# Front of a gated-loop layer: phase angles by Ln, Exp and a Newton step, integer phases, and another order of the stages ahead of the expert tiles

## The chip, the cores and the metric

The kernel runs on one core of one Trainium2 chip. The metric is the time of one execution on the device in microseconds (us), as the median of several runs. A core has five engines that work side by side, each with an instruction stream of its own: PE (matrix products into PSUM banks), DVE (vector work), ACT (activation functions, copies), POOL (vector work and, here, the issue of gathers and scatters) and SP (the issue of other DMAs). They wait for each other by semaphores. ACT keeps a table of functions; where the next function isn't in it, the program has an instruction ACT_TABLE_LOAD.

## The reference, cut to what matters

Two layers over 2048 tokens of 128 numbers. Each adds to its input an attention part and a feed-forward part, both of the normed input. The change touches the first layer alone.

```python
# first layer, attention: xn is the normed, scaled input of one sequence of 512 tokens
q = xn @ wq; k = xn @ wk; v = xn @ wv; a = xn @ wa; g = xn @ wg
a_r, a_i = jnp.split(a, 2, axis=-1)
a_c = lax.complex(a_r, a_i)
magnitude = jax.nn.sigmoid(jnp.abs(a_c))
phase = jnp.angle(a_c)
a_c = magnitude * jnp.exp(1j * phase)
# y[t] = a_c[t] * y[t-1] + k[t] * v[t], over the sequence
y = q * jnp.real(y)
y = y * jax.nn.silu(g)
return y @ wo
# first layer, feed-forward: two of eight experts for every token
h1 = x_rep @ w1[e].T
a, g = jnp.split(h1, 2, axis=-1)
he = jax.nn.silu(a) * g @ w2[e].T
out = out * scores.reshape(-1, 1)
combined = out.reshape(N, TOP_K, h).sum(axis=1)
# second layer: a state-space scan and 64 experts, eight for every token
```

## The kernel before, in words

The tokens lie in NB = 4 blocks of TB = 512, one sequence each; a tile of the attention is 128 features by 512 tokens. The kernel is written by engine: five functions (SP, POOL, ACT, DVE, PE) that each issue their instructions in the order of the text, with waits on counting semaphores. Tables of Python numbers say at which place a step stands: `PROJ` is the order of the 24 projections on PE with the PSUM bank of each, `FR_ACT` and `FR_DVE` count the steps of the front, `FR_BESIDE`, `BACK_AT` and `BACK_STEPS` say beside which tile of the loop a step of the attention is issued.

*The angle of a block.* PE makes the products ar and ai (L315 to L317, three matmuls each, since numbers are split in a high and a low part). ACT copies and squares both (L730 to L734), DVE adds the squares and bounds the sum (L1080, L1082), ACT takes the square root (L745), which is |a|, and Abs of ar (L742, L756). The angle is twice the arctangent of ai / (|a| + |ar|), turned by sign where ar is negative. DVE adds (L1091), takes the reciprocal in two halves (L1092, L1094) and multiplies (L1095). ACT then makes Sigmoid of |a| (L762) and Arctan (L763), `angle(b)`. DVE makes two numbers from the sign of ar (L1098, L1099) and from them and the arctangent the angle in turns, split in a part rounded to a fine grid and a rest (`turn`, L1102 to L1106). Both parts are summed along the sequence by scans in float (`whole` L1159, `rest` L1161); `wrap` (L1164 to L1166) takes whole turns off.

*The rest of the attention.* ACT makes sines of the phase in two steps (`sin` L770 to L772, `double` L774 and L776). DVE turns k * v back by the phase (`spin`), runs a real and an imaginary decay scan (`fall_i`, `fall_r`), turns the sum forward and multiplies it by q * silu(g) (`sum`); PE multiplies by wo; DVE adds (`add`). Block b begins these steps at tile `BACK_AT[b]` of the loop below.

*The experts.* From a routing table, 39 tiles of 128 token slots of one expert each are made. DVE writes one-hot tables, PE multiplies them: L1495 makes the table of tokens (32 products of 128x78), L1503, at step 5 of the second half of the projections, that of the weights (32 products of 128x117). DVE turns the first into row numbers (L1115 to L1120) and the second into `weight` (L1140 to L1142). Then the tile loop runs, n from -2. For each tile POOL gathers 128 rows by an indirect DMA (`fetch`, L563, ten tiles ahead), PE turns the rows (L1444), ACT copies the high part (L783), DVE takes the low part (L1190), PE makes the two halves of the hidden layer (L1455 to L1461), ACT takes Silu (`tile_silu`, L790), DVE multiplies (`gate`, L1198), PE turns the result (L1471), ACT copies it (L797), PE makes the output (L1482), ACT weighs it (`weigh_out`, L806) and POOL scatters it by an indirect DMA (`send`, L582). Four buffers t_out stand between ACT and POOL. From tile 27 on POOL prepares weights of the second layer in between (`prepare`). The second layer begins behind the last scatter.

*What the change touches around it.* In `angle`, blocks 0 and 1 come ahead of the first tile's Silu and blocks 2 and 3 at tile 14 (`ANGLES_AT`). POOL splits the projection weights first, then those of the experts, and spreads the lane numbers in two pieces between (`spread_lanes`, L548). It gathers five tiles, waits for the weights table, clears three pads and gathers five more.

## Time and profile before

| what | value |
|---|---|
| median of 3 runs | 439.59 us (439.34 to 443.05) |
| the profiled execution | 439.73 us |
| its span on the core | 437.98 us, shown as 438.0 |
| busy: PE, DVE, ACT, POOL | 331.7, 352.8, 263.1, 247.3 us |

The span is the time from the first instruction to the last on the core; 1.75 us of the execution lie outside it. Busy time is the sum over a whole span with stages of different kinds, so a share of it tells nothing of a stage. In a row of a timeline the first number is the start in us from the span's start, the second the duration; in brackets at the end stands how long the engine had been idle before, and what ended that wait.

### The profile page before, as it was taken

The numbers are of one execution on the slowest core, as the hardware profiler recorded it, in microseconds if no ns is written. First come the engines' busy times: TensorE is split into PE (matmuls) and PEld (weight loads), VectorE is DVE, ScalarE is ACT, GpSimd is POOL, SyncE is SP. The second block draws the span as 40 slices with busy tenths as digits, with TensorE's granted clock in tenths as the row PEclk, the third lists the DMA queues.
The fourth block names the chain that finished last, engine by engine and source line by source line (L and its number), as shares of the span: only waits on it lengthen the run. The fifth ranks groups of instructions, "written<-read, shape, count | busy, mean of one in ns | idle before, by whom it ended". The sixth has DMA issues, their size and how long they took to land. (4 is left out here: it accounts for less than half of the span.)

```text
span 438.0 us, 5588 instructions
## 1 busy us (share of the span) xinstructions
PE 331.7 (76%) x1491; PEld 233.4 (53%) x1491; DVE 352.8 (81%) x623; ACT 263.1 (60%) x443; POOL 247.3 (56%) x254
## 2 busy tenths in 40 slices
PE   0855698927798698989702986979798888988875
PEld 0535466717786596877601553535455554545453
DVE  5869999899799597959229677888999988988955
ACT  2477596072757657575512589768668578678320
POOL 5486602510587377778830000058988988889850
PEclk9996698675999799999955999899999999999999
DMA  6365300100111111311060002004778866755973
GB/s 174 91 186 139 82 0 8 36 18 0 38 44 49 31 43 49 91 46 36 25 204 6 1 1 48 0 7 91 138 149 159 159 130 136 150 109 103 180 151 96
DMA packets 36212, 35.09 MB, mean 80 GB/s; under 512 B 12165, under 2 KB 30838, under 8 KB 36182
## 3 DMA queue, kind: packets, MB, share of 16 engines
q0 software_dynamic: 7104, 21.90, 24.1%
q1 hardware_dynamic: 29078, 12.84, 10.9%
q8 instruction: 14, 0.23, 0.2%
q14 instruction: 16, 0.13, 0.1%
HBM read 13.29 MB, written 4.65 MB: 41 GB/s over the span
## 5 line engine op out<-in xcount | busy, mean ns | idle before, releaser
L1301 DVE TENSOR_TENSOR_SCAN state<-dec,win_t 128x1024 f32<-128x1024 f32 x32 | 83.7, 2637 | 2.4 <-ACT dec L862 1.4
L871 ACT ACTIVATE sil<-psum,vec_t 128x512 f32<-128x512 f32 x64 | 43.2, 687 | 44.3 <-PE psum L317 44.2
L635 POOL TENSOR_SCALAR state<-state,ssm_cb 128x1024 f32<-128x1024 f32 x32 | 63.2, 1975 | 2.5 <-POOL sel_now L612 2.5
L582 POOL DMA_INDIRECT parts<-t_out,part x39 | 41.0, 1052 | 40.0 <-ACT t_out L806 30.2
L563 POOL DMA_INDIRECT x_tile<-normed,token x39 | 41.3, 1059 | 32.5 <-DVEq L1120 20.3
L1630 PE MATMUL psum<-hid,g_w 128*128 128x512 f32 x128 | 59.5, 592 | 0.0
L1312 DVE TENSOR_TENSOR hid<-sil,psum 128x512 f32<-128x512 f32 x64 | 41.7, 677 | 14.5 <-ACT sil L871 8.2
L1622 PE MATMUL psum<-cw_hl,sel_now 128*128 128x512 f32 x64 | 36.6, 572 | 16.6 <-DVE hid L1312 13.9
L797 ACT ACTIVATE t_hid_t<-psum 128x384 f32<-128x384 f32 x39 | 19.2, 492 | 31.2 <-PE psum L1471 31.2
L622 POOL MEMSET dec<- 128x4 f32 x6 | 0.6, 104 | 64.2 <-DVEq L1269 50.4
L1198 DVE TENSOR_TENSOR t_hid<-t_sil,psum 128x352 f32<-128x352 f32 x39 | 20.3, 521 | 19.4 <-ACT t_sil L790 16.6
L1630 PEld LDWEIGHTS psum<-hid,g_w 128*128 128x128 f32 x128 | 24.2, 189 | 20.3 <-issue 18.0
L1482 PE MATMUL psum<-w_out,t_hid_t 128*128 x234 | 33.8, 282 | 1.1 <-ACT t_out L806 0.9
L642 POOL DMA_DIRECT2D xn_tok<-state x32 | 28.7, 898 | 10.2 <-POOL state L635 8.4
L862 ACT ACTIVATE dec<-dt_t,ssm_a 128x2044 f32<-128x2044 f32 x16 | 31.1, 1992 | 3.9 <-DVEq L1269 3.8
L1482 PEld LDWEIGHTS psum<-w_out,t_hid_t 128*128 128x128 f32 x234 | 30.2, 197 | 1.8 <-issue 1.7
L1444 PE MATMUL psum<-ident,x_tile 128*128 128x128 f32 x39 | 12.4, 317 | 23.2 <-DVE xt_lo L1190 21.1
L1622 PEld LDWEIGHTS psum<-cw_hl,sel_now 128*128 128x128 f32 x64 | 12.0, 188 | 31.9 <-DVE hid L1312 23.8
L315 PE MATMUL psum<-xn_hi,g_hi 128*128 128x512 f32 x64 | 25.8, 403 | 3.0 <-ACT sil L871 3.0
L316 PE MATMUL psum<-xn_hi,g_lo 128*128 128x512 f32 x64 | 25.3, 395 | 0.0
L317 PE MATMUL psum<-xn_lo,g_hi 128*128 128x512 f32 x64 | 25.2, 394 | 0.0
L1455 PE MATMUL psum<-w_hi,xt_hi 128*128 x78 | 25.0, 405 | 0.0
(316 smaller groups left out, 860.0 us busy)
## 6 DMA issues: line engine op xcount, KB each, us to landing
xn_tok<-state POOLq DMA_DIRECT2D x32, 512.0 KB, 4.7
e_raw<-in_L_ffn_w SPq DMA_DIRECT2D x16, 128.0 KB, 2.2
both<-parts SPq DMA_DIRECT2D x4, 512.0 KB, 5.1
e_raw<-in_L_ffn_w SPq DMA_DIRECT2D x8, 176.0 KB, 2.5
res<-in_L_attn_x SPq DMA_DIRECT2D x4, 256.0 KB, 3.5
normed<-rows SPq DMA_DIRECT2D x1, 1024.0 KB, 5.5
g_raw<-in_L_ffn_w SPq DMA_DIRECT2D x16, 64.0 KB, 2.2
g_w<-in_L_ffn_w SPq DMA_DIRECT2D x16, 64.0 KB, 2.4
```

What stands on the lines that cost most here:

```text
L315: pe.matmul(acc, w_hi, m_hi, start=True, stop=False)
L563: pool.indirect_dma_start(out=x_tile[n % XRING][:, :], out_offset=None, in_=normed, in_offset=bass.IndirectOffsetOnAxis(ap=token[:, n:n + ...
L582: pool.indirect_dma_start(out=parts, out_offset=bass.IndirectOffsetOnAxis(ap=part[:, n:n + 1], axis=0), in_=t_out[n % ORING][:, :], in_off ...
L635: own(pool.tensor_scalar(state[k % 4][:, :], state[k % 4][:, :], ssm_cb[:, k // 2:k // 2 + 1], 0.0, ALU.mult, ALU.add))
L642: pool.dma_start(y_t[:, (k % 2) * HALF:(k % 2 + 1) * HALF], state[k % 4][:, :], accum_op=ALU.add).then_inc(y_in[k % 4], 16)
L862: act.activation(dec[n % DECS][:, :].rearrange("p (b t) -> p b t", t=TB)[:, :, 1:TB], dt_t[:, :].rearrange("p (b t) -> p b t", t=TB)[:, :, ...
L871: act.activation(sil[c % SRING][:, :], ps[c % 2][:, :], ACT.Silu, bias=vec_t[:, V_B1 + c // NBLK:V_B1 + c // NBLK + 1]).then_inc(h_silu, 1)
L1301: dve.tensor_tensor_scan(state[k % 4][:, :], dec[(k // 2) % DECS][:, at_half], win_t[:, at_half], 0.0, ALU.mult, ALU.add).then_inc(scanned, 1)
L1312: dve.tensor_tensor(hid[c % HRING][:, :], sil[c % SRING][:, :], ps[2 + c % 2][:, :], ALU.mult).then_inc(hid_done, 1)
L1482: ins = pe.matmul(ps[O_BANK][:, 0:P], t_hid_t[n % 2][:, c * P:(c + 1) * P], w_out[:, e, c, :].rearrange("p a d -> p (a d)"), start=(c == 0 ...
L1622: pe.matmul(ps[2 + c % 2][:, :], sel_now[g % GRING][:, :], blk(cw_hl, tb), start=True, stop=True).then_inc(cwx_made, 1)
L1630: pe.matmul(ps[4 + tb][:, :], g_w2[g % GRING][:, :], hid[c % HRING][:, :], start=False, stop=g == NG - 1, skip_group_check=True).then_inc( ...
```

## The change

**Angles.** The reciprocal leaves DVE. DVE adds |ar| to |a| (`den`), ACT takes Ln and then Exp with a scale of -1 of the sum, block by block (`over`), and DVE makes one Newton step and the product (`tan`, three operations). All four Abs stand ahead of the square roots. The sign of ar is taken by ACT (Sign, with a tiny bias) instead of two DVE operations.

**Place of the angles.** All four blocks' Sigmoid and Arctan stand ahead of the first tile's Silu (n = -2 and -1); none is left at tile 14.

**Phases.** An angle is counted in 2^15 to a turn. The scan `whole` writes integers, `wrap` is a bitwise and and one more operation. The sine is taken as a shifted sine and its square in one ACT step of four operations; `spin`, `fall_i`, `fall_r`, `back` and `sum` on DVE have 8 operations for 9. The steps of a block's back part fall from 15 DVE operations to 12 and from 5 ACT operations to 4.

**Order and banks.** `PROJ` has another order: k and v of block 0 and k of block 1 come ahead of ar and ai of blocks 2 and 3, and q of block 3 goes to the bank that g of block 0 had. The weights table stands behind all projections. DVE makes the sums of squares and the token table ahead of the products of k and v, and the weights from the weights table (`leave_weights`) inside the tile loop at n = 0. ACT spreads the lane numbers in four pieces. POOL splits the projection weights behind expert 3 and gathers all ten tiles at once. Waits that stood ahead of the tile loop on PE stand inside it.

The diff, cut:

```diff
-                [("k", 2, 6), ("v", 2, 7), ("k", 3, 2), ("v", 3, 3), ("g", 1, 4), ("q", 1, 0), ("g", 2, 4), ("q", 2, 1),
-                 ("g", 3, 4), ("q", 3, 5)])
...
+                [("k", 2, 6), ("v", 2, 0), ("k", 3, 5), ("v", 3, 1), ("g", 1, 6), ("q", 1, 5), ("g", 2, 4), ("q", 2, 0),
+                 ("g", 3, 1), ("q", 3, 3)])
...
-        ANGLES_AT = 14
+        FR_ACT_AT = {-2: [("angle", 0), ("angle", 1)], -1: [("sign", 0), ("angle", 2), ("angle", 3)], 1: [("sign", 1)],
+                     2: [("sign", 2)], 4: [("sign", 3)]}
+        FR_BESIDE = {-2: [("tan", 2), ("q", 2)], -1: [("tan", 3), ("q", 3)], 0: [("turn", 0)], 3: [("turn", 1)],
+                     12: [("turn", 2)], 22: [("turn", 3)]}
...
-        BACK_OPS = {"whole": 1, "rest": 1, "wrap": 3, "spin": 2, "fall_i": 2, "fall_r": 2, "sum": 3, "add": 1}
+        BACK_OPS = {"whole": 1, "rest": 1, "wrap": 2, "spin": 2, "fall_i": 1, "fall_r": 1, "back": 2, "sum": 2, "add": 1}
...
-            pool.wait_ge(proj_in, 16 * 6)
-            split(proj_raw[:, :, :], proj_hi[:, :, :], proj_lo[:, :, :])
-            pool.nop().then_inc(weights_split, 1)
-            def spread_lanes(half):
...
-                if e in (LANES_AT, 3):
-                    pool.wait_ge(qkv_t_made, NBLK)
-                    spread_lanes(int(e == 3))
+                if e == 3:
+                    pool.wait_ge(proj_in, 16 * 6)
+                    split(proj_raw[:, :, :], proj_hi[:, :, :], proj_lo[:, :, :])
+                    pool.nop().then_inc(weights_split, 1)
...
-            for n in range(AHEAD // 2):
+            for n in range(AHEAD):
                 fetch(n)
...
+            def spread_lanes(n):
+
+                lo, hi = n * P // LANES, (n + 1) * P // LANES
+                own(act.activation(lane_p[:, lo:hi, :], lane[:, lo:hi, None].to_broadcast([P, P // LANES, NSEL]), ACT.Copy))
+                act.nop().then_inc(lanes_ready, 1)
...
-            step(act.activation(held["q"][0], held["ar"][0], ACT.Abs))
+            for b in BLOCKS:
+                step(act.activation(held["q"][b], held["ar"][b], ACT.Abs))
             for b in BLOCKS:
                 act.wait_ge(fr_dve, FR_DVE["m2", b])
                 step(act.activation(held["decay"][b], t1[b], ACT.Sqrt))
-            act.wait_ge(table_made, 1)
+            leave_key(2)
+            leave_key(3)
             for b in BLOCKS:
+                act.wait_ge(fr_dve, FR_DVE["den", b])
+                step(act.activation(held["q"][b], t1[b], ACT.Ln))
+                step(act.activation(held["q"][b], held["q"][b], ACT.Exp, scale=-1.0))
+            for b in BLOCKS:
+                act.wait_ge(fr_pe, FR_PE["g", b])
                 if b == 2:
-                    act.wait_ge(weights_made, 1)
-                act.wait_ge(fr_pe, FR_PE["g", b])
+                    act.wait_ge(weights_hot, 1)
                 step(act.activation(t2[b], ps[FR_BANK["g", b]][:, :], ACT.Silu))
...
+                    step(act.activation(t2[b], held["ar"][b], ACT.Sign, bias=least[:, 0:1]))
...
+                step(act.activation(turn_cos[:, :], th, ACT.Abs))
+                step(act.activation(turn_sin[:, :], th, ACT.Sin, scale=math.pi / TURN, bias=eighth[:, 0:1]))
+                step(act.activation(turn_sin[:, :], turn_sin[:, :], ACT.Square))
+                step(act.activation(k, turn_cos[:, :], ACT.Sin, scale=-2.0 * math.pi / TURN, bias=half_pi[:, 0:1]))
...
-                if n == ANGLES_AT:
-                    for b in (2, 3):
-                        angle(b)
+                for name, b in FR_ACT_AT.get(n, ()):
+                    angle(name, b)
...
+                    dve.wait_ge(fr_act, FR_ACT["over", b])
+                    step(dve.tensor_tensor(t1[b], t1[b], q, ALU.mult))
+                    step(dve.scalar_tensor_tensor(t1[b], t1[b], 2.0, q, ALU.subtract, ALU.mult))
+                    step(dve.tensor_tensor(t1[b], ai, t1[b], ALU.mult))
...
-                    step(dve.reciprocal(t1[b][:, half[0]], den[:, half[0]]))
...
-                    step(dve.tensor_tensor_scan(k, ones[:, :], ar, 0.0, ALU.mult, ALU.add))
+                    step(dve.tensor_tensor_scan(k.bitcast(mybir.dt.int32), ones[:, :], ar, 0.0, ALU.mult, ALU.add))
...
-                    step(dve.tensor_scalar(ar, k, ROUND_INT, ROUND_INT, ALU.add, ALU.subtract))
-                    step(dve.tensor_tensor(k, k, ar, ALU.subtract))
-                    step(dve.tensor_tensor(th, k, th, ALU.add))
+                    step(dve.tensor_scalar(whole, whole, int(TURN) - 1, None, ALU.bitwise_and))
+                    step(dve.scalar_tensor_tensor(th, whole, TURN / 2, th, ALU.subtract, ALU.subtract))
...
                 for name, b in FR_BESIDE.get(n, ()):
-                    turn_part(name, b)
+                    front(name, b)
+                if n == 0:
+                    leave_weights()
...
-            for at_step, (name, b, bank) in enumerate(PROJ[1]):
-                if at_step == WEIGHTS_AT:
-                    weights_table()
+            for name, b, bank in PROJ[1]:
                 project(name, b, bank)
+            pe.wait_ge(weights_hot, 1)
+            for c in range(NSEL):
+                ins = pe.matmul(ps[TABLE_BANK][:, 2 * NTILE:5 * NTILE], slot_hot[:, :, c], tile_hot[:, 0:3, :, c],
+                                start=c == 0, stop=c == NSEL - 1)
+            ins.then_inc(weights_made, 1)
```

What the diff doesn't show at once is where the table loads of ACT stand, which the compiled program decides. The instructions of ACT, before, from the square roots to the last Abs (`at_all` holds |a|, `for_front` and `front` the front's scratch, `kept` the attention's tiles, `xt_hi` a tile of rows):

```order
L745 ACT_TABLE_LOAD
L745 ACTIVATE at_all<-for_front 128x512 x4
L751 ACT_TABLE_LOAD
L751 ACTIVATE for_front<-psum 128x512
L738 ACTIVATE kept_51<-psum 128x512
L738 ACTIVATE kept_52<-psum 128x512
L751 ACTIVATE for_front<-psum 128x512
L751 ACTIVATE front_140<-psum 128x512 x2
L756 ACTIVATE front_140<-at_all 128x512 x3
L783 ACTIVATE xt_hi_66<-psum 128x128
```

The same place in the changed kernel, from the square roots on; the last row begins block 1, and blocks 1 to 3 have four rows like the four of block 0; behind them come a load and the four Silus:

```order
L751 ACT_TABLE_LOAD
L751 ACTIVATE at_all<-for_front 128x512 x4
L743 ACTIVATE kept_51<-psum 128x512
L743 ACTIVATE kept_52<-psum 128x512
L756 ACT_TABLE_LOAD
L756 ACTIVATE kept_93<-for_front 128x512
L757 ACT_TABLE_LOAD
L757 ACTIVATE kept_93<-kept_93 128x512
L756 ACT_TABLE_LOAD
```

Between the square roots and the Silus there was one load. Now eight more stand there, one ahead of each Ln (L756) and each Exp (L757), and all Silus are behind them.

PE, before, at the weights table (L1503) in the middle of the projections:

```order
L317 MATMUL psum<-xr_lo,proj_hi 128x512
L1503 MATMUL psum<-tile_hot,slot_hot 128x117 x32
L315 MATMUL psum<-xr_hi,proj_hi 128x512
L316 MATMUL psum<-xr_hi,proj_lo 128x512
L317 MATMUL psum<-xr_lo,proj_hi 128x512
```

PE, changed, the last projection, the weights table (L1512) and the first turn of a tile (L1448):

```order
L317 MATMUL psum<-xr_hi,proj_hi 128x512
L318 MATMUL psum<-xr_hi,proj_lo 128x512
L319 MATMUL psum<-xr_lo,proj_hi 128x512
L1512 MATMUL psum<-tile_hot,slot_hot 128x117 x32
L1439 TENSOR_LOAD tile_e
L1439 ISA x2
L1448 MATMUL psum<-ident,x_tile_54 128x128
```

The table stood between two projections with five more behind it; now it stands between the last projection and the first tile.

DVE, before, from the low part of tile 2 to the gating of tile 0 (L1198):

```order
L1190 TENSOR_TENSOR xt_lo_71<-psum,xt_hi_68 128x128
L1102 TENSOR_TENSOR for_front<-for_front,front_140 128x512
L1103 SCALAR_TENSOR_TENSOR for_front<-for_front 128x512
L1105 TENSOR_SCALAR at_all<-for_front 128x512
L1106 TENSOR_TENSOR at_all<-for_front,at_all 128x512
L1159 SCALAR_TENSOR_TENSOR turn_k_86<-ones,at_all 128x512
L1198 TENSOR_TENSOR t_hid_74<-t_sil_72,psum 128x352
```

DVE, changed, from the same low part to the same gating (now L1196):

```order
L1188 TENSOR_TENSOR xt_lo_71<-psum,xt_hi_68 128x128
L1098 SCALAR_TENSOR_TENSOR for_front<-front_140,for_front 128x512
L1100 TENSOR_SCALAR at_all<-for_front 128x512
L1101 SCALAR_TENSOR_TENSOR at_all<-at_all,for_front 128x512
L1102 SCALAR_TENSOR_TENSOR at_all<-front_140,at_all 128x512
L1142 SCALAR_TENSOR_TENSOR spare<-part_f,spare 128x39
L1143 SCALAR_TENSOR_TENSOR part<-part_f,spare 128x39
L1146 COPY weight<-psum 128x39
L1147 TENSOR_TENSOR weight<-weight,psum 128x39
L1148 TENSOR_TENSOR weight<-weight,psum 128x39
L1157 SCALAR_TENSOR_TENSOR turn_k_86<-ones,at_all 128x512
L1196 TENSOR_TENSOR t_hid_74<-t_sil_72,psum 128x352
```

The turn of block 1 gave way to that of block 0 (the turn of block 0 stood ahead of the low part before), and the five operations on the weights stand between it and the scan.

## Rows read from the trace of the kernel before

**Rows 1.** Windows: length, busy of PE, PEld, DVE, ACT, POOL; clock, DMA share, GB/s.

```profile
0.00:53.20 53.20, 26.82 (x143) 20.20 (x144) 40.95 (x139) 27.84 (x61) 34.39 (x46) 0.85 0.50 138
89.60:111.10 21.50, 12.94 (x52) 11.44 (x53) 19.80 (x31) 9.98 (x21) 0.48 (x1) 0.60 0.02 5
111.10:221.50 110.40, 91.76 (x607) 80.24 (x605) 82.61 (x142) 70.68 (x174) 82.04 (x76) 0.96 0.16 46
```

**Rows 2.** Groups of POOL from 111.1 to 221.5: scatters and gathers, idle time before.

```profile
L582 POOL DMA_INDIRECT parts<-t_out,part x39 | 41.0, 1052 | 40.0 <-ACT t_out L806 30.2 <-issue 8.2 <-POOL sw_lo L540 0.8
L563 POOL DMA_INDIRECT x_tile<-normed,token x29 | 31.4, 1083 | 9.0 <-issue 7.3 <-PE psum L1444 1.2 <-POOL ssm_cb L592 0.5
```

**Rows 3.** Waits of POOL: us in total, times, the longest.

```profile
POOL parts L582 <- ACT t_out L806: 30.2, 8, 21.1
```

**Rows 4.** Timeline of POOL: three of the 39 scatters.

```profile
111.16 1.00 POOL L582 DMA_INDIRECT parts<-t_out,part  x1 [21.07 <-ACT t_out L806]
...
148.68 1.19 POOL L582 DMA_INDIRECT parts<-t_out,part  x1 [4.00 <-ACT t_out L806]
...
220.51 0.97 POOL L582 DMA_INDIRECT parts<-t_out,part  x1 [0.31 <-issue]
```

**Rows 5.** Timeline of ACT at tile 14: both table loads.

```profile
141.91 1.28 ACT L762 ACT_TABLE_LOAD   x1
...
145.84 1.28 ACT L790 ACT_TABLE_LOAD   x1
```

**Rows 6.** Timeline of PE at the end of the front.

```profile
76.16 6.56 PE L1503 MATMUL psum<-tile_hot,slot_hot 128*128 128x117 bf16 x32 [1.11 <-DVEq L1129]
...
86.86 0.40 PE L315 MATMUL psum<-xr_hi,proj_hi 128*128 128x512 f32 x1
...
87.33 0.40 PE L317 MATMUL psum<-xr_lo,proj_hi 128*128 128x512 f32 x1
89.61 0.33 PE L1444 MATMUL psum<-ident,x_tile 128*128 128x128 f32 x1 [1.88 <-DVE front L1091]
```

**Rows 7.** Timeline of ACT in the front.

```profile
53.24 0.60 ACT L730 ACTIVATE at_all<-psum 128x512 f32<-128x512 f32 x1 [1.96 <-POOLq L554]
...
63.60 1.23 ACT L738 ACTIVATE kept<-psum 128x512 f32<-128x512 f32 x2
64.87 0.63 ACT L742 ACTIVATE kept<-at_all 128x512 f32<-128x512 f32 x1
67.91 1.28 ACT L745 ACT_TABLE_LOAD   x1 [2.41 <-DVE for_front L1082]
...
72.14 1.28 ACT L751 ACT_TABLE_LOAD   x1
73.43 0.60 ACT L751 ACTIVATE for_front<-psum 128x512 f32<-128x512 f32 x1
...
90.35 1.28 ACT L762 ACT_TABLE_LOAD   x1
...
98.39 0.46 ACT L790 ACTIVATE t_sil<-psum 128x352 f32<-128x352 f32 x1 [0.19 <-PE psum L1461]
```

**Rows 8.** Timeline of DVE: a reciprocal, a turn's operation, a scan, the first gating.

```profile
78.83 1.75 DVE L1092 RECIPROCAL for_front<-kept 128x256 f32<-128x256 f32 x1
...
96.57 0.69 DVE L1103 SCALAR_TENSOR_TENSOR for_front<-for_front 128x512 f32<-128x512 f32 x1
...
101.32 1.22 DVE L1159 TENSOR_TENSOR_SCAN turn_k<-ones,at_all 128x512 f32<-128x512 f32 x1
102.58 0.52 DVE L1198 TENSOR_TENSOR t_hid<-t_sil,psum 128x352 f32<-128x352 f32 x1
```

**Rows 9.** Timeline of ACT in the second layer: Exp, Square, a load ahead of Ln.

```profile
261.72 1.06 ACT L884 ACTIVATE pair<-pair 128x1024 f32<-128x1024 f32 x1
...
264.89 2.56 ACT L891 ACTIVATE at_all<-at_all,half_mid 128x512 f32<-128x512 f32 x4
267.46 1.28 ACT L894 ACT_TABLE_LOAD   x1
```

More of the change, by code:

```diff
@@ L15 @@
 TB = 512
-ROUND_TURN = 1.5 * 2.0 ** 10
+TURN = 2.0 ** 15
+QUARTER = TURN / 4
 ROUND_INT = 1.5 * 2.0 ** 23
@@ L364, in program @@
         BACK_AT = (0, 9, 19, 28)
[L365 to L367 removed]
+        BACK_STEPS = {"whole": 0, "rest": 1, "wrap": 2, "sin": 3, "spin": 4, "fall_i": 5, "fall_r": 6, "back": 7, "sum": 8,
+                      "wo": 9, "add": 10}
+        BACK_OPS = {"whole": 1, "rest": 1, "wrap": 2, "spin": 2, "fall_i": 1, "fall_r": 1, "back": 2, "sum": 2, "add": 1}
@@ new lines, in _ @@
+            for b in BLOCKS:
+                front("m2", b)
+            dve.wait_ge(table_made, 1)
+            of_lane, of_row = (ps[TABLE_BANK][:, n * NTILE:(n + 1) * NTILE] for n in range(2))
+            own(dve.tensor_copy(part_f[:, :], of_lane))
+            own(dve.scalar_tensor_tensor(part_f[:, :], of_row, float(P * TOPK), part_f[:, :], ALU.mult, ALU.add))
+            own(dve.tensor_scalar(token_f[:, :], part_f[:, :], -1.0, 0.5, ALU.min, ALU.mult))
+            own(dve.tensor_scalar(token_f[:, :], token_f[:, :], -0.25, ROUND_INT, ALU.add, ALU.add))
@@ L1063, in _ @@
+            own(dve.tensor_scalar(token[:, :], token_f[:, :], ROUND_INT - NTOK, None, ALU.subtract))
+            dve.nop().then_inc(token_ready, 1)
+            front("kv", 0)
+            front("kv", 1)
+            for b in BLOCKS:
+                front("den", b)
             own(dve.tensor_tensor_scan(counts[:, 0, :], ones[0:1, 0:NTILE], ones[0:1, 0:NTILE], 0.0, ALU.mult, ALU.add))
```

245 lines of the change are left out of this document (107 added, 138 removed).

## The prediction

> **What bounds the kernel now.** I read the stages first. The windows [rows 1] cut the span into a front to 53.2 us, a rest of the front, a first-tile stage from 89.6, the loop of 39 tiles from 111.1 to 221.5, and the second layer. In the loop POOL is busy for 82.04 of 110.4 us, in 76 instructions. PE is busier, so the next view is who waits for whom. POOL's groups [rows 2] show 39 scatters and 29 gathers, 1.05 and 1.08 us each, with a fixed gap of 0.30 us that the profile calls "issue" between nearly all of them. The waits [rows 3] show eight scatters that waited for ACT's t_out, 30.2 us in all, of which 21.1 is the first. The other seven took 9.1 us; 7 x 0.30 is the usual gap, so 7.0 us are true waiting. The timeline [rows 4] places 3.70 of it at 148.68 (4.00 less 0.30), behind the stall of ACT at 141.91: a table load, four angle instructions and a load back [rows 5]. So the loop is POOL's queue of issues: from the first scatter at 111.16 to the last at 220.51 are 109.35 us, of which 7.0 are waits for a late t_out and 102.35 are POOL's own.
>
> Ahead of it stands the front. PE's first turn of a tile begins at 89.61 [rows 6], ACT's first Silu of a tile at 98.39 [rows 7], the first gating multiply on DVE at 102.58 [rows 8], the first scatter at 111.16: 8.78, 4.19 and 8.58 us. In that stage the granted clock of PE averaged 0.60, so it ran mostly at its lower level of 1.2 GHz; in the loop it averaged 0.96, nearly all at 2.4 GHz [rows 1]. Whatever delays the first scatter delays the last, unless POOL's 7.0 us of waiting absorb it. The second layer follows the last scatter and isn't changed.
>
> **The change part by part, in the time of the trace.** *Start of the front.* POOL's two spreads go to ACT, in four Copies of 128x1024; the nearest row of that size takes 1.06 us [rows 9], so 4.2 us. ACT is busy for 27.84 of the first 53.2 us, and still waits 1.96 for POOL at 53.24 [rows 1, 7]. POOL's projection split moves behind expert 3, into time that the spreads free. I take 0, between -0.4 and +1.1 (one Copy uncovered).
>
> *ACT up to the Silus.* The 16 copies and squares still take 10.36 us (53.24 to 63.60), plus 0.45, since three more projections stand ahead of block 2 on PE: 64.05. Two k: 65.3. Four Abs instead of one, at 0.66 (0.63 and a gap of 0.03) [rows 7]: 67.95. A load and four Sqrts, 3.95 by their rows less the 0.33 or so of waiting: 71.9. Two k: 73.15. Now what is new: for each block Ln, then Exp, and in the order of the changed kernel each of these eight has a table load ahead of it. A load takes 1.28 us, and the next instruction starts 0.01 to 0.02 later [rows 5, 7]. The trace shows no Ln or Exp of 128x512; the nearest are Abs and Silu of that size, 0.63 and 0.60, and Exp of twice the size, 1.06. I take 0.66 with its gap (0.6 to 1.1 as bounds). 8 x (1.30 + 0.66) = 15.7: 88.85. A load and Silu 0: 90.8. In the kernel before Silu 0 was done at 74.03.
>
> That the loads are truly paid shows at the second layer, where Exp, Square and Ln follow and Ln has a load of 1.28 us of its own at 267.46 [rows 9]. The Trainium skill, "ScalarE: Activation LUTs", section "Table sets: the hidden batching unit", says that Ln after Exp needs one load, because one set has both. By that rule seven of the eight loads fall away (rival 1); the row at 267.46 speaks against it.
>
> *PE.* The last projection, q of block 3, now goes to the bank that g of block 0 holds until Silu 0 has read it, so it starts at 90.9 and takes 0.9 (86.86 to 87.73 before). Behind it stands the weights table, moved from the middle of the projections; it took 6.2 to 6.6 us at half clock [rows 6]. PE has idled before it again: 6.3, ending at 98.1 (3.2 at full clock is the lower bound). Queued behind it are the first turns of tiles: turn 0 at 98.2 instead of 89.61, +8.6. The 1.88 us that this turn waited for DVE go.
>
> *DVE of the front.* Eight reciprocals of 1.75 us go, 14.0 us [rows 8]; Newton steps bring 12 instructions of 0.69, 8.3 us, two of the four behind the projections' end. ACT ends later than DVE here, so this saves nothing by itself.
>
> *First tiles.* From turn 0 on ACT does its copy, a load, eight angle instructions (four before) and a Sign, a load back, and the first tile Silu. That is 10.4 us instead of 8.78: two blocks more at 1.32 and 0.66 for the Sign, less waits of 1.6 that were there: 108.6. Then DVE: the integer turn of block 0 (2.6 us), the five small table operations, moved here (1.1), and the integer scan stand ahead of gate 0; they begin at 107.6, at the last tile copy, and end at 112.6. For the integer scan I take 1.25 as for the float one, 2.4 at most (the same scan twice). Gate 0 at 112.8 instead of 102.58, 4.2 behind the Silu as before. From there to the first scatter were 8.58; wrap has one operation less on DVE, 0.7: 7.9, if PE stays at half clock as in this stage before. The first scatter: 120.7, +9.5.
>
> *The loop.* The stall at 141.91 is gone, with the DVE reciprocals around it. With no late t_out the chain is POOL's own, 102.35. New is about 0.8 at the second scatter, since block 0's scan and turn 1 lie between gates 0 and 2. Fewer DVE operations run beside POOL's issues: per block 12 instead of 15 in the back part. POOL's issues have 0.97 at their shortest (220.51 [rows 4]), so 39 x 0.08 + 29 x 0.11 = 6.3 us are lengthening; where it comes from no view says. I take 1.0 of it off (0 to 2.7). The Trainium skill, "GPSIMD Engine Reference", section "1. Specifications", names a shared SBUF interface with VectorE as a place of contention with two-input instructions; no row here isolates it. Last scatter: 120.7 + 102.35 + 0.8 - 1.0 = 222.9, against 220.51: +2.4.
>
> The profiled execution took 439.73 us, 437.98 of it the span. It stands 0.14 above the median of the runs, 439.59. So 439.59 + 2.4 = 442.0 us.
>
> **The rivals.**
> 1. *Faster: one load for Ln and Exp.* If one load serves both functions, seven loads of 1.30 are not paid, and the 15.7 become 6.6. Turn 0 comes at 89.1 and the first scatter at 111.6; the last is at 111.6 + 102.15 = 213.8, -6.7: 432.9 us. It is decided as soon as four of the seven fall away. Against it stand the program's eight loads and the load before Ln [rows 9]. This is the rule of the Trainium skill named above. Chance 0.05.
> 2. *The loop pays everything back.* PE is busy for 0.60 of the first-tile stage [rows 1]; of the 7.9 us to the first scatter that is 4.7, and at full clock up to 2.4 are saved. I take 1.8: 118.9. POOL loses 2.7 of lengthening instead of 1.0. Last scatter 118.9 + 102.35 + 0.8 - 2.7 = 219.4, -1.1: 438.5 us. For it: DVE's work beside POOL shrinks. Against: the first tiles ran at half clock before. Chance 0.28, of which 0.03 for sums under 435.2 (a weights table at full clock, 3.1 earlier, and a start 0.4 earlier on top).
> 3. *Slower: the late start is kept and DVE becomes the bound of the first tiles.* If PE stays at half clock through the first four tiles, while DVE still owes turn 1, the scan, the wrap and the spin, scatters 2 to 5 wait for t_out again: about 2.5 us in all. With no relief for POOL (+1.0) this is 2.4 + 1.0 + 2.5 = +5.9: 445.5 us. It is slower by over 1% once these two terms reach 2.0. For it: 19.80 of 21.5 us DVE busy in that stage [rows 1]. Against: POOL waited for only 7.0 us in the whole loop before, most of it at the stall. Chance 0.28.
> 4. *Each load costs twice its row.* If loads that alternate cost as much again as the 1.28 of their row, the eight more of them ahead of the first scatter add 10.2: 452.2 us. Against it: the instruction behind the load at 72.14 starts at 73.43 [rows 7]. The section "What ACT_TABLE_LOAD costs" of that ScalarE page gives some 1.38 us of drain to each switch beside the load; the trace doesn't agree, by those 0.01 us. Chance 0.01.
> 5. *The change doesn't do what it says.* The stall at tile 14 stays, or the angles wait elsewhere in the loop: then the 3.7 aren't won: +6.1, 445.7 us, counted in rival 3's 0.28.
>
> **How the numbers follow.** The forecast has 0.38, rival 2 0.28, rival 3 0.28, rival 1 0.05, rival 4 0.01. A measurement of this kernel tells about 1% from no change, so 435.2 and 444.0 are the bounds. Slower: rival 3 and 4, 0.29; faster: rival 1 and the 0.03, 0.08; same: the rest, 0.63. The range goes from 437.0, just under rival 2, to 447.0, above rival 3; the scan at 2.4 us and an uncovered Copy lie in it. The forecast's own range is 440.5 to 444.
>
> **What would show it.** In the profile of the changed kernel: eight loads of 1.28 us at the Ln and Exp lines, Silu 0 of the front near 90; the weights table near 92 to 98 and turn 0 at 98.2; the first tile Silu at 108.6; the first scatter at 120 to 121; no load between the first tile and the last; waits of POOL for t_out behind the first scatter of 1 to 3 us instead of 7.0; the last scatter near 223. Wrong would be: fewer loads, a turn 0 before 92, or a last scatter before 219 or after 226. If the front is late by 9 and the end by none, POOL's lengthening was the term that I sized too small.

## The result and the profile after

The changed kernel takes 448.84 us (448.51 to 450.78, four runs) against 439.82 us: a ratio of 1.0207, 95% interval 1.0175 to 1.024. It is slower by some 2% (the interval reaches to both sides of 1.02), and outside the range of the prediction (437.0 to 447.0). Each time in this document is the median of a kernel's fast runs, since some executions take some per cent longer at a lower granted clock. Its profiled execution has a span of 447.2 us against 438.0. Cut at the same events, the 9.2 us come from these stages:

| stage | before | changed | difference | predicted |
|---|---|---|---|---|
| to ACT's first copy of ar | 53.24 | 50.12 | -3.12 | 0 |
| from there to turn 0 on PE | 36.37 | 45.26 | +8.89 | +8.6 |
| turn 0 to the first scatter | 21.55 | 22.97 | +1.42 | +0.9 |
| first to last scatter | 109.35 | 108.21 | -1.14 | -7.1 |
| last scatter to the end | 217.47 | 220.64 | +3.17 | 0 |

ACT's timeline (start, duration, instruction; in brackets the idle time before) answers to [rows 7]:

```profile
50.12 0.60 ACT L735 ACTIVATE at_all<-psum 128x512 f32<-128x512 f32 x1 [1.96 <-POOLq L548]
...
64.84 1.28 ACT L751 ACT_TABLE_LOAD   x1
...
70.03 1.28 ACT L756 ACT_TABLE_LOAD   x1
71.33 0.63 ACT L756 ACTIVATE kept<-for_front 128x512 f32<-128x512 f32 x1
71.98 1.28 ACT L757 ACT_TABLE_LOAD   x1
73.27 0.63 ACT L757 ACTIVATE kept<-kept 128x512 f32<-128x512 f32 x1
...
85.57 1.28 ACT L762 ACT_TABLE_LOAD   x1
86.86 1.23 ACT L762 ACTIVATE front<-psum 128x512 f32<-128x512 f32 x2
...
105.83 0.46 ACT L797 ACTIVATE t_sil<-psum 128x352 f32<-128x352 f32 x1
```

The eight loads are there, 1.28 us each, with 0.63 us of Ln or Exp between; block 0's pair stands at 70.03 to 73.90, and three more pairs follow until the load for Silu at 85.57. Ln starts 0.02 us behind its load, and the next load 0.02 us behind Ln, so the drain of some 1.38 us that the Trainium skill, "ScalarE: Activation LUTs", section "What ACT_TABLE_LOAD costs", gives beside a load isn't seen here. The stage to turn 0 is on PE's timeline, which answers to [rows 6]:

```profile
76.90 0.80 PE L317 MATMUL psum<-xr_hi,proj_hi 128*128 128x512 f32 x1 [5.10 <-DVE kept L1075]
...
87.51 0.79 PE L317 MATMUL psum<-xr_hi,proj_hi 128*128 128x512 f32 x1 [7.69 <-ACT front L762]
...
88.96 6.59 PE L1512 MATMUL psum<-tile_hot,slot_hot 128*128 128x117 bf16 x32
95.38 0.39 PE L1448 MATMUL psum<-ident,x_tile 128*128 128x128 f32 x1
```

PE waits for DVE's products of blocks 2 and 3, then 7.69 us for Silu 0, makes q of block 3, and then the weights table in 6.59 us, at its lower clock. Turn 0 follows it directly. The first-tile stage ran at a granted clock of 0.50, so all at 1.2 GHz, and the loop at 0.93 (windows: length, busy time of PE, PEld, DVE, ACT and POOL, clock, DMA share, GB/s; before in [rows 1]):

```profile
90.00:111.00 21.00, 11.06 (x45) 8.00 (x43) 11.86 (x24) 10.76 (x18) 0.37 (x3) 0.50 0.00 0
118.30:227.50 109.20, 89.33 (x607) 81.87 (x605) 68.92 (x126) 64.24 (x165) 85.96 (x76) 0.93 0.17 46
```

The loop is where the forecast broke. POOL's groups, its waits and three of its issues answer to [rows 2 to 4]:

```profile
L575 POOL DMA_INDIRECT parts<-t_out,part x39 | 43.3, 1111 | 36.1 <-ACT t_out L813 25.9 <-issue 8.5 <-POOL sw_lo L543 0.8
L558 POOL DMA_INDIRECT x_tile<-normed,token x29 | 32.3, 1114 | 9.0 <-issue 7.6 <-PE psum L1448 0.9 <-POOL ssm_cb L585 0.5
```

```profile
POOL parts L575 <- ACT t_out L813: 25.9, 7, 22.2
```

```profile
118.35 1.34 POOL L575 DMA_INDIRECT parts<-t_out,part  x1 [22.25 <-ACT t_out L813]
...
163.35 1.90 POOL L575 DMA_INDIRECT parts<-t_out,part  x1 [0.31 <-issue]
...
226.56 0.97 POOL L575 DMA_INDIRECT parts<-t_out,part  x1 [0.30 <-issue]
```

The waits for t_out did go as forecast: seven, 25.9 us, of which 22.25 is the first; the other six take 3.65, less 6 x 0.30 is 1.85 us, against 7.0 before. But a scatter now takes 1.11 us in the mean and a gather 1.11, against 1.05 and 1.08. An issue that no operation of DVE holds up takes 0.96 to 1.01 us, most often 0.99 (scatter) and 0.97 (gather). What it takes beyond these two I call lengthening: it is 39 x 0.121 + 29 x 0.144 = 8.9 us; by the same measure it was 39 x 0.062 + 29 x 0.113 = 5.7 in [rows 2]. POOL's own chain without waits is 108.21 - 1.85 = 106.3 us instead of 102.4: 3.2 us of that are lengthening, 0.7 are weight preparations of POOL that took longer. The longest issue, 1.90 us at 163.35, began 0.11 us behind a scan on DVE, whose timeline has it, beside the first integer scan:

```profile
108.72 1.23 DVE L1157 TENSOR_TENSOR_SCAN turn_k<-ones,at_all 128x512 int32<-128x512 f32 x1
...
163.24 1.22 DVE L1159 TENSOR_TENSOR_SCAN turn_th<-ones,at_all 128x512 f32<-128x512 f32 x1
```

The integer scan takes 1.23 us, as the one in float ([rows 8]). The scan at 163.24 ends at 164.46 and the scatter at 165.25, 0.79 later.

A product on DVE that reads two tensors from SBUF, the core's other on-chip memory beside PSUM, does the same to an issue that starts inside it. In the changed kernel, DVE's product first, then POOL's gather, which ends 0.84 us behind the product:

```profile
130.19 0.69 DVE L1176 SCALAR_TENSOR_TENSOR at_all<-turn_sin,at_all 128x512 f32<-128x512 f32 x1
```

```profile
130.29 1.43 POOL L558 DMA_INDIRECT x_tile<-normed,token  x1 [0.30 <-PE psum L1448]
```

An issue that starts late in a scan loses nothing. In the kernel before, one starts 1.01 us behind the start of a scan and takes 1.00:

```profile
187.54 1.22 DVE L1161 TENSOR_TENSOR_SCAN turn_th<-ones,at_all 128x512 f32<-128x512 f32 x1
```

```profile
188.55 1.00 POOL L563 DMA_INDIRECT x_tile<-normed,token  x1 [0.30 <-issue]
```

In both traces an issue starts inside 13 of the 14 scans of the loop. Before, five of the 13 start in a scan's last 0.22 us and one together with it, and seven are lengthened; in the changed kernel twelve are. Sorted by what DVE is at when an issue starts, the 5.7 us of before are 3.3 in scans and 2.4 in such products, and the 8.9 us of now are 6.6, 2.0 and 0.4 in other operations, less 0.2 where an issue took a little less than 0.99 or 0.97.

### The profile page after: what moved, and what is told of

It reads as the page before. It is cut to its first block and busy times, and to the rows that moved or that the text cites. A ratio compares the mean times of both kernels' runs of the same rounds, so it can differ in the third digit from the quotient of the medians.

```text
span 447.2 us, 5607 instructions
## 1 busy us (share of the span) xinstructions
PE 333.8 (75%) x1491; PEld 238.5 (53%) x1491; DVE 332.1 (74%) x607; ACT 280.3 (63%) x461; POOL 248.8 (56%) x254
## 5 line engine op out<-in xcount | busy, mean ns | idle before, releaser
L575 POOL DMA_INDIRECT parts<-t_out,part x39 | 43.3, 1111 | 36.1 <-ACT t_out L813 25.9
L1631 PE MATMUL psum<-hid,g_w 128*128 128x512 f32 x128 | 60.4, 599 | 0.0
L558 POOL DMA_INDIRECT x_tile<-normed,token x39 | 43.5, 1115 | 29.0 <-DVEq L1114 17.3
L1196 DVE TENSOR_TENSOR t_hid<-t_sil,psum 128x352 f32<-128x352 f32 x39 | 20.3, 521 | 29.2 <-ACT t_sil L797 19.8
L1492 PE MATMUL psum<-w_out,t_hid_t 128*128 x234 | 34.8, 288 | 1.0 <-ACT t_out L813 0.9
L1492 PEld LDWEIGHTS psum<-w_out,t_hid_t 128*128 128x128 f32 x234 | 31.3, 203 | 1.7 <-issue 1.7
L1448 PE MATMUL psum<-ident,x_tile 128*128 128x128 f32 x39 | 12.5, 320 | 20.9 <-DVE xt_lo L1188 18.1
L1359 PE MATMUL psum<-ident,xn_tok 128*128 128x128 f32 x32 | 7.7, 433 | 25.1 <-DVE xn_tok L1230 25.1
```

The source lines that it names most:

```text
L558: pool.indirect_dma_start(out=x_tile[n % XRING][:, :], out_offset=None, in_=normed, in_offset=bass.IndirectOffsetOnAxis(ap=token[:, n:n + ...
L575: pool.indirect_dma_start(out=parts, out_offset=bass.IndirectOffsetOnAxis(ap=part[:, n:n + 1], axis=0), in_=t_out[n % ORING][:, :], in_off ...
L1492: ins = pe.matmul(ps[O_BANK][:, 0:P], t_hid_t[n % 2][:, c * P:(c + 1) * P], w_out[:, e, c, :].rearrange("p a d -> p (a d)"), start=(c == 0 ...
L1631: pe.matmul(ps[4 + tb][:, :], g_w2[g % GRING][:, :], hid[c % HRING][:, :], start=False, stop=g == NG - 1, skip_group_check=True).then_inc( ...
```

## The experiments

All ratios are to the kernel before, measured on the same chip beside them. "Start" is ACT's first copy of ar; it stands at 50.1 in the changed kernel, and between 49.2 and 52.0 in the eleven other traces of kernels that begin the same way. So stages are best compared from the start.

**Two loads instead of eight.** Ln of all blocks, then Exp of all:

```diff
                 step(act.activation(held["q"][b], t1[b], ACT.Ln))
+            for b in BLOCKS:
                 step(act.activation(held["q"][b], held["q"][b], ACT.Exp, scale=-1.0))
```

> The changed kernel with Ln of all four blocks ahead of Exp of all four: two table loads instead of eight, nothing else moved. If ACT's loads set the front, six loads of 1.30 us (7.8) go: turn 0 of PE at 87.6 instead of 95.4, first scatter at 110.6 instead of 118.4, and if the loop keeps its length the time falls by about 7.8 to 441 us. If another engine stands right behind ACT, turn 0 moves by less than 3 us and the time stays above 446.

441.33 us, ratio 1.0031 (1.0004 to 1.0058). ACT and PE in its trace:

```profile
70.06 1.28 ACT L756 ACT_TABLE_LOAD   x1
71.35 2.62 ACT L756 ACTIVATE kept<-for_front 128x512 f32<-128x512 f32 x4
73.98 1.28 ACT L758 ACT_TABLE_LOAD   x1
75.28 2.61 ACT L758 ACTIVATE kept<-kept 128x512 f32<-128x512 f32 x4
```

```profile
80.66 6.55 PE L1513 MATMUL psum<-tile_hot,slot_hot 128*128 128x117 bf16 x32
87.03 0.39 PE L1449 MATMUL psum<-ident,x_tile 128*128 128x128 f32 x1
```

Turn 0 stands at 87.03, 8.4 us earlier, the first scatter at 109.45, the last at 218.73, 7.8 us earlier. The time is 7.5 us lower, so six needless loads are most of the changed kernel's 9.0. Put beside the rule of the Trainium skill ("ScalarE: Activation LUTs", "Table sets: the hidden batching unit"): its advice to group calls by set holds, while its example, one load for Ln and then Exp, isn't what these programs have; they have a load at each change between the two.

**The weights table ahead of the last projection.**

```diff
-            for name, b, bank in PROJ[1]:
+            for at_step, (name, b, bank) in enumerate(PROJ[1]):
+                if at_step == 9:
+                    ...
                 project(name, b, bank)
-            pe.wait_ge(weights_hot, 1)
...
```

> The changed kernel with the weights table on PE ahead of the last projection (q of block 3) instead of behind it; the eight loads stay. PE idles from 79.8 to 87.5 there, and the table takes 6.4. If the table's place costs its full length, turn 0 comes at 89.0 instead of 95.4, first scatter near 112, time about 442.5 us. If the first turn waits for something else too, it moves by less than 2 us and the time stays above 447.

443.28 us, ratio 1.0100 (1.0058 to 1.0143). PE:

```profile
79.02 6.57 PE L1512 MATMUL psum<-tile_hot,slot_hot 128*128 128x117 bf16 x32
88.38 0.79 PE L317 MATMUL psum<-xr_hi,proj_hi 128*128 128x512 f32 x1 [2.79 <-ACT front L762]
...
89.83 0.41 PE L1448 MATMUL psum<-ident,x_tile 128*128 128x128 f32 x1
```

The table lies in the time in which PE waits for Silu 0, and turn 0 follows q of block 3 at 89.83: 5.6 us earlier, as expected to 0.8.

**Both**, the table ahead of q of block 2.

> Both edits together, the table ahead of q of block 2. The two overlap, since without the loads PE no longer idles as long: turn 0 at 86, first scatter at 109, 9.4 us earlier than in the changed kernel, time 439 to 440 us. If the loop's own length (106.3 us of POOL's issues) is what is lost, the time stays about 4 us above a front as early as that of the kernel before would give.

438.65 us, ratio 0.9966 (0.9897 to 1.0035): turn 0 at 86.99, first scatter at 110.05 from a start at 51.76. The first rival of the prediction, worked out as 432.9, had its first scatter 1.6 us later, at 111.6; still this run ends some 6 us behind it. Its loop takes 109.05 us, of which 107.2 are POOL's own, where the rival had 102.15.

**The projection split back at the front of POOL.**

```diff
-                if e == 3:
-                    pool.wait_ge(proj_in, 16 * 6)
-                    split(proj_raw[:, :, :], proj_hi[:, :, :], proj_lo[:, :, :])
-                    pool.nop().then_inc(weights_split, 1)
...
+            pool.wait_ge(proj_in, 16 * 6)
+            split(proj_raw[:, :, :], proj_hi[:, :, :], proj_lo[:, :, :])
+            pool.nop().then_inc(weights_split, 1)
             for e in range(E0):
```

> The changed kernel with POOL's split of the projection weights put back ahead of the experts' splits; ACT keeps the four spreads. If the place of that split gave the front its early start, ACT's first copy of ar comes near 53 us again instead of 50.1 and all behind it is 3 us later: turn 0 near 98.4, time near 451.5 us. If the spreads' move to ACT gave it, the first copy stays within 0.5 of 50.1.

One run, 451.56 us. POOL at the start, DVE's normalisation of the input rows beside it, and ACT's first copy:

```profile
12.74 0.94 POOL L542 TENSOR_SCALAR proj_hi<-proj_raw 128x768 fp32r<-128x768 f32 x1 [3.63 <-DMA wo_sb<-in_L_attn_wo]
13.77 1.80 POOL L543 TENSOR_TENSOR proj_lo<-proj_raw,proj_hi 128x768 fp32r<-128x768 f32 x1
```

```profile
10.51 6.42 DVE L943 TENSOR_SCALAR rows<-res,mv,nrm 128x128 f32<-128x128 f32 x16 [0.15 <-DVE nrm L940]
```

```profile
54.00 0.60 ACT L734 ACTIVATE at_all<-psum 128x512 f32<-128x512 f32 x1 [2.07 <-POOLq L551]
```

The front starts at 54.0 instead of 50.1, so the place of the split gave the early start. POOL's wait of 3.63 us for the weights isn't itself what the front loses; it puts the split beside DVE's normalisation. DVE's row in the changed kernel, where POOL splits nothing before 17.8:

```profile
10.48 4.20 DVE L944 TENSOR_SCALAR rows<-res,mv,nrm 128x128 f32<-128x128 f32 x16 [0.15 <-DVE nrm L941]
```

Fourteen of the sixteen operations take 0.34 us in both; the two that stand beside the split, from 12.8 to 15.7, take 0.93 and 1.98. So the normalisation, which the front needs, ends 2.2 us later. The kernel before has the same 6.42 us there. What makes the other 1.6 of the 3.9 us wasn't traced.

**The same part alone, on the kernel before** (the split moved behind expert 3, the spreads left on POOL).

> The kernel before with that one part alone: POOL splits the projection weights behind expert 3, and keeps its spreads. POOL waited 3.9 us for the projection weights at the start, so the front should start 1 to 3 us earlier than 53.2, and the time fall to 437 to 438.5 us. If POOL's spreads of 3.8 us take that time instead, the start stays at 53 and the time at 439.6.

438.95 us, ratio 0.9945 (0.991 to 0.998). DVE's normalisation takes 4.20 us here too, and the start came at 51.35, 1.9 us earlier. The time falls by 1.2 us by the medians and 2.4 by the ratio. This part of the change is good by itself.

**The reciprocal back on DVE**, in place of Ln, Exp and the Newton step:

```diff
-                    dve.wait_ge(fr_act, FR_ACT["over", b])
-                    step(dve.tensor_tensor(t1[b], t1[b], q, ALU.mult))
-                    step(dve.scalar_tensor_tensor(t1[b], t1[b], 2.0, q, ALU.subtract, ALU.mult))
+                    step(dve.reciprocal(t1[b], t1[b]))
                     step(dve.tensor_tensor(t1[b], ai, t1[b], ALU.mult))
```

> The changed kernel with the reciprocal back on DVE (one of 128x512 a block, about 3.5 us) in place of Ln, Exp and the Newton step; all else as changed. ACT has no new loads, DVE 14.0 + 2.8 us instead of 8.3. Turn 0 near 87.5, but tan of blocks 2 and 3 then stands between the low parts of the first tiles: first Silu of a tile near 100, first scatter near 112.5 instead of 118.4, time near 443 us. So even the old reciprocal would beat eight loads; it would lose some 3 us to the version with two loads (first scatter 109.5). If it comes at 109 or earlier, Ln and Exp bring nothing at all.

442.16 us, ratio 1.0048 (1.0015 to 1.0082): turn 0 at 87.51, first tile Silu at 100.69, first scatter at 113.29 from a start at 51.68. So the old reciprocal beats eight loads by 6.7 us, and with two loads Ln and Exp bring the first scatter 1.8 us nearer to the start than it (59.84 from start to first scatter against 61.61). The times of the two, 442.16 and 441.33, don't tell them apart: their intervals overlap.

**One tensor read in place of two.** In the back part of the attention every scan and two-tensor operation on DVE becomes an operation on one tensor, for example:

```diff
-                    step(dve.tensor_tensor_scan(ai, decay, two, 0.0, ALU.mult, ALU.add))
+                    step(dve.tensor_scalar(ai, two, 1.0, 0.0, ALU.mult, ALU.add))
```

> The changed kernel with every scan and two-tensor operation of the back part on DVE replaced by an operation on one tensor of the same shape (it leaves out the recurrences and products of the attention). Theory: POOL's issue of an indirect DMA is held up by a DVE operation that reads two tensors in SBUF. Then issues stay at 0.97 to 1.00 us, the 8.9 us of lengthening in the loop fall below 2, the last scatter comes about 98 us behind the first instead of 108, and the time is near 439 us. Rival: the lengthening comes from DMA traffic or from DVE being busy at all: then at least 5 us of it stay.

440.19 us, ratio 0.9996 (0.9953 to 1.0039), where near 439 was expected. The first scatter is at 116.54, the last at 218.77; POOL's issues:

```profile
L575 POOL DMA_INDIRECT parts<-t_out,part x39 | 39.5, 1013 | 36.5 <-ACT t_out L813 26.3 <-issue 8.5 <-POOL sw_lo L543 0.8
L558 POOL DMA_INDIRECT x_tile<-normed,token x29 | 29.1, 1004 | 9.0 <-issue 6.4 <-PE psum L1448 2.1 <-POOL ssm_cb L585 0.5
```

The lengthening falls from 8.9 to 39 x 0.023 + 29 x 0.034 = 1.9 us. The chain without waits is 98.2 us; the waits are 4.0, so the last scatter comes 102.2 us behind the first, not 98. These operations are also shorter, which leaves a second reading open; the next run closes it.

**One tensor read, but as long as a scan.** At each scan's place, for example:

```diff
+                    own(dve.reciprocal(th[:, 0:178], ones[:, 0:178]))
                     step(dve.tensor_scalar(ai, two, 1.0, 0.0, ALU.mult, ALU.add))
```

> As the run with one-input operations, but each of the four scans of a block is replaced by a reciprocal of 128x178 (about 1.2 us, the length of a scan, one tensor read) ahead of the short operation; the attention's recurrences and products are left out again. It tells the two readings apart that are left: if two tensors read from SBUF hold POOL's issue up, the lengthening in the loop stays below 3 us and POOL's own chain at 98 to 99 us. If any long DVE operation does, it returns to 7 us or more and the chain to 104 or more.

One run, 441.18 us. POOL's groups, then one of the reciprocals on DVE and the issue of POOL that starts inside it:

```profile
L575 POOL DMA_INDIRECT parts<-t_out,part x39 | 39.3, 1009 | 37.8 <-ACT t_out L813 27.8 <-issue 9.2 <-POOL sel L592 0.6
L558 POOL DMA_INDIRECT x_tile<-normed,token x29 | 28.7, 989 | 9.0 <-issue 6.4 <-PE psum L1452 2.1 <-POOL ssm_cb L585 0.5
```

```profile
147.50 1.26 DVE L1173 RECIPROCAL turn_th<-ones 128x178 f32<-128x178 f32 x1
```

```profile
148.13 0.97 POOL L558 DMA_INDIRECT x_tile<-normed,token  x1 [0.30 <-issue]
```

The issue at 148.13 starts 0.63 us into a reciprocal that ends at 148.76, and takes 0.97 us. Twelve of the 14 reciprocals meet an issue, and all twelve issues take 0.96 to 1.00. In the changed kernel issues that start as far inside a scan take 1.4 to 1.5. The lengthening is 39 x 0.019 + 29 x 0.019 = 1.3 us and the chain 97.2. So DVE being busy doesn't hold POOL's issue up; scans and products that read two tensors from SBUF do. Two tensors of which one lies in PSUM don't: in the changed kernel 18 issues start inside such an operation, and none is lengthened. The Trainium skill, "GPSIMD Engine Reference", section "1. Specifications", names this contention with two SBUF inputs; the runs agree, and give its price. One tensor isn't always free, though: an issue at 130.95 of this run starts 0.06 us into a TENSOR_SCALAR of 0.42 us on one tensor and takes 1.21. That is where most of the 1.3 us come from.

**A version meant to beat both.** Two loads; the weights table ahead of g of block 3; q of blocks 2 and 3 behind the first turn; the count of tiles behind the products of k and v.

```diff
+                if at_step == 7:
+                    pe.wait_ge(weights_hot, 1)
...
                     turn_x(n + 2)
+                if n == -2:
+                    for name, b, bank in PROJ[1][8:]:
+                        project(name, b, bank)
```

> A version meant to beat both: two loads for Ln and Exp, the weights table ahead of g of block 3, q of blocks 2 and 3 behind the first turn of a tile, the count of tiles on DVE behind the products of k and v. Turn 0 at 82.5, first Silu of a tile at 93, first scatter at 105, last at 213 to 215 with the loop's own 107; time 431 to 435 us. If g of block 3 or the third Silu holds turn 0 back it comes at 85 to 87, and the time is that of the version with both edits, 438 to 439.

434.94 us, ratio 0.9886 (0.9824 to 0.9947): turn 0 at 81.90, first tile Silu at 92.79, first scatter at 105.35, last at 214.43. The front came within 0.6 us of what was worked out, and POOL's own chain stayed long at 107.2 us:

```profile
L575 POOL DMA_INDIRECT parts<-t_out,part x39 | 44.8, 1149 | 37.6 <-ACT t_out L814 26.8 <-issue 9.1 <-POOL sw_lo L543 0.8
L558 POOL DMA_INDIRECT x_tile<-normed,token x29 | 32.4, 1117 | 9.0 <-issue 7.6 <-PE psum L1451 0.9 <-POOL ssm_cb L585 0.5
```

**Its angles of blocks 2 and 3 back at tile 14.** The turn of block 2 moves with them, from tile 12 to tile 18.

> The reordered version with the angles of blocks 2 and 3 put back at tile 14. Ahead of the first tile four angle instructions of 0.66 and a wait of 0.6 go: first scatter 3 us earlier, near 102.3. In the loop the two table loads and four instructions come back: POOL waits for t_out rise from 1.9 to 6 or 7 us. Sum: the last scatter 1 to 3 us later than in the reordered version, time 436 to 438 us. If the front gives more than the stall takes, it is not slower, and moving the angles ahead was no gain.

434.57 us, ratio 0.9881 (0.9839 to 0.9923): no difference, where 1 to 3 us were expected. The first scatter is 3.6 us nearer to the start (52.1 against 55.7). The waits came back as expected, 30.4 us less 21.1 for the first and 7 x 0.30 are 7.2, but the lengthening fell from 10.5 to 6.5 us:

```profile
POOL parts L575 <- ACT t_out L814: 30.4, 8, 21.1
```

```profile
L575 POOL DMA_INDIRECT parts<-t_out,part x39 | 41.9, 1073 | 39.8 <-ACT t_out L814 30.4 <-issue 8.5 <-POOL sel L592 0.6
L558 POOL DMA_INDIRECT x_tile<-normed,token x29 | 31.4, 1084 | 9.0 <-issue 8.5 <-POOL ssm_cb L585 0.5
```

First to last scatter are 109.6 us, 109.1 with the angles ahead. So moving the angles ahead of the loop, the part of the change from which I expected the gain, brought nothing in this version: what it saves in waits it loses in lengthening and in the front.

**PE kept busy ahead of the second layer** by 24 products with no use.

> The reordered version with 24 matrix products of 128x512 (about 20 us, results unused) on PE between its last output and the second layer, where it waits 25 us. If the clock that falls in that wait costs the second layer its start, the stretch from the last scatter to the end shrinks from 218.3 to 215 to 217 us and the time from 434.9 to 432 to 433.5. If the clock there is not on the path, the time stays; if the products run at the lower clock they end late and it is slower by up to 15 us.

434.88 us, ratio 0.9863 (0.9835 to 0.9892), against 434.94 without: no difference. From 226 to 232 us the granted clock was 1.00 with the products and 0.50 without, and the last scatter to the end took 219.7 us, not less than 218.3. The clock in that wait is not on the path. That theory fell.

**The back steps paired as before:** one product, then product and imaginary scan, then real scan and product.

```diff
-        BACK_OPS = {"whole": 1, "rest": 1, "wrap": 2, "spin": 2, "fall_i": 1, "fall_r": 1, "back": 2, "sum": 2, "add": 1}
+        BACK_OPS = {"whole": 1, "rest": 1, "wrap": 2, "spin": 1, "fall_i": 2, "fall_r": 2, "back": 1, "sum": 2, "add": 1}
...
```

> The reordered version with the back steps on DVE paired as in the kernel before: one product, then product and imaginary scan, then real scan and product, then one product; the same operations. In the reordered version 13 of 14 scans in the loop are met by the start of an issue of POOL, which then waits for the scan's end (10.4 us of lengthening, POOL's own chain 107.2). If the place of a scan in its tile decides that, the lengthening falls to 6 to 8 us, the chain to 103 to 105 and the time by 2 to 4 us. If it is the number of two-input operations alone, which stays, the chain stays at 106.5 to 108 and the time at 434.9.

432.69 us, ratio 0.9811 (0.9783 to 0.9839). Every run behind this median is shorter than every one of the reordered version (432.94 at most, 433.74 at least). POOL's groups:

```profile
L575 POOL DMA_INDIRECT parts<-t_out,part x39 | 41.7, 1070 | 36.2 <-ACT t_out L814 26.5 <-issue 8.8 <-POOL sel L592 0.6
L558 POOL DMA_INDIRECT x_tile<-normed,token x29 | 30.9, 1065 | 9.0 <-issue 8.2 <-POOL ssm_cb L585 0.5 <-PE psum L1451 0.3
```

The lengthening falls from 10.5 to 39 x 0.080 + 29 x 0.095 = 5.9 us and the chain to 102.5, with the same operations. Thirteen issues start inside a scan in both versions. What differs is how much of the scan is left at that moment: 13 of them are lengthened in the reordered version, by 7.5 us, and 10 here, by 4.3. The issues that start inside products lose 1.1 us instead of 2.6. So the place of these operations within a tile sets the price. This is the best version of the study.

**The changed kernel a second time.**

> The changed kernel once more, for a second trace of it. In its first trace the second layer, which the change leaves alone, took 220.6 us from the last scatter to the end, against 217.5 before and 217.8 in the run with the split first; 2.5 of it were stretches at 1.2 GHz. If that belongs to this program, it is 220 to 221 again with the same two stretches. If it is the run's, it comes at 217.5 to 219 or with other stretches, and the change itself costs some 6.5 us and not 9.

One run, 446.77 us. Start, turn 0, first and last scatter are where they were within 0.4 us (50.09, 95.23, 118.20, 226.97), but the second layer takes 218.0 us instead of 220.6. Windows of both traces, at its start and near its end, the changed kernel's first trace first:

```profile
244.80:252.80 8.00, 7.77 (x25) 4.76 (x25) 7.57 (x21) 5.37 (x10) 0.00 (x0) 0.50 0.00 0
426.50:431.00 4.50, 4.50 (x10) 2.56 (x9) 0.94 (x2) 1.38 (x2) 2.51 (x3) 0.62 0.92 174
```

```profile
245.20:252.20 7.00, 6.56 (x25) 4.04 (x25) 6.58 (x20) 5.37 (x10) 0.00 (x0) 0.70 0.00 0
427.00:431.50 4.50, 4.50 (x17) 3.03 (x17) 2.02 (x3) 1.37 (x2) 1.46 (x2) 1.00 1.04 197
```

The clock was 0.50 and 0.62 in the first trace where it was 0.70 and 1.00 in the second. These 2.6 us are not the program's: the same program ran without them. What brought them stays open: all four earlier runs took 448.5 us or more, and this is a single later one.

## Why the prediction was wrong

- **The front: right.** ACT's eight loads, Silu 0 as the release of the last projection, the weights table behind it and turn 0: predicted +8.6 us from the start, measured +8.89. Ln and Exp took the 0.63 us that I had taken for them, plus a gap of 0.02. Runs with two loads and with the table elsewhere moved turn 0 by 8.4 and 5.6, so both causes are shown, and they overlap.
- **The first tiles: right.** Predicted 22.5 us from turn 0 to the first scatter, measured 22.97; its three parts are 10.45, 4.15 and 8.37, against 10.4, 4.2 and 7.9. The integer scan costs no more than the old one.
- **The start: wrong, the other way.** I took the move of the split and the spreads as 0, between -0.4 and +1.1; it was -3.1. I looked at POOL's busy time and missed whom its split holds up. The trace of before shows the split at 12.63, behind a wait for a DMA:

```profile
12.63 0.94 POOL L539 TENSOR_SCALAR proj_hi<-proj_raw 128x768 fp32r<-128x768 f32 x1 [3.86 <-DMA wo_sb<-in_L_attn_wo]
```

  Beside it DVE's normalisation takes 6.42 us, and 4.20 without it. The two traces with the split first start at 53.2 and 54.0, the thirteen with the split behind expert 3 between 49.2 and 52.0.
- **The loop: the step that failed.** "With no late t_out the chain is POOL's own, 102.35" and "I take 1.0 of it off". The waits fell by 5.1 us, as forecast to 1 us. But 102.35 held 5.7 us of lengthening (6.3 by the measure used there) that I let fall with the number of DVE operations. (A block's back part has 13 after the change, not 12 as I counted, against 15.) It goes by how much is left, when an issue of POOL starts, of a DVE operation that holds it. There are four scans a block before and after, and an issue starts inside 13 of the 14 in the loop in both; 7 were lengthened before and 12 after, their share rose from 3.3 to 6.6 us, and the chain became 106.3. Fewer products did help as I thought, but by 0.4 us. From POOL's minimum the step was mis-sized by 5.0 us (-1.0 taken, +4.0 measured), and by 6.0 with the 0.8 us of new waiting that came as 1.85. Rival 3, slower because of late t_out in the first tiles, named another place and is not what happened: those waits are 1.85 us. Its term "no relief for POOL" was nearer than mine, but still put at nothing what became +4.0. Rival 2 rested on the opposite sign of the same term.
- **The tail: not seen.** I let everything behind the last scatter shift alike. It took 3.2 us more in the first trace; 2.6 of that were stretches at the lower clock that the second trace doesn't have. The rest, some 0.6 us, stays open: every trace of a kernel derived from the changed one has a tail that is 0.3 us or more longer than before.
- The sum: the misses of -3.1 (start), +0.3, +0.5, +6.0 (loop) and +3.2 (tail) make, but for rounding, the 6.8 us between +2.4 and +9.2. The early start hid half of the loop's miss, which was luck. By the second trace the change costs 446.77 - 440.41 (the kernel before beside it), 6.4 us.

What stays open: why issues start later in the scans when the back steps are paired as before. The runs show that the place of the scans and products decides the price, not a rule by which a place could be chosen ahead.

## What to carry to other kernels

Count the table loads in the compiled order, not in the text: a loop over blocks with two functions in it paid a load for every instruction, and splitting the loop in two took six of eight away. Where a queue of issues bounds a loop, its own time is no constant: look what DVE does while an issue starts, and price a removed wait only after asking what the queue meets instead. And ask of a step on an idle engine what runs beside it: POOL had time for its split, but the split cost DVE, and with it the front, 2.2 us.

## What the runs showed of the hardware that I had not expected

An indirect DMA issue of POOL that starts inside a scan on DVE ends 0.77 to 0.82 us behind the scan's end, however early it began: 1.90 us when it began 0.11 behind the scan's start, 1.54 when 0.47 behind, 1.30 when 0.72 behind. One that begins in the scan's last 0.2 us takes its usual time. Inside a product of 0.69 us on two tensors in SBUF the same holds, with an end 0.84 to 0.89 us behind the product's. When an issue and a scan start within 0.03 us of each other the issue takes its usual time and the scan is longer instead, 1.27 to 1.29 us. A reciprocal of 1.26 us, which reads one tensor, holds no issue up. The other way round, POOL's split of 128x768 held up two of DVE's operations of 0.34 us, which read one tensor of 128x128: they took 0.93 and 1.98. Sign with a bias tile took 0.71 to 0.74 us for 128x512, where Sigmoid without one took 0.63.
